# Routing of a mixture-of-experts layer: logits turned inside the second gate, the exponential ahead of the gate's activation, and row scatters sorted by choice

## The reference, cut to what matters

```python
logits = h @ gate_weight.T                              # 1024 tokens x 8 experts
scores = softmax(logits)
topk_w, topk_i = _group_limited_topk(scores)            # 2 of 4 groups of 2 experts, then 2 experts
wmat = (one_hot(topk_i, 8) * topk_w[..., None]).sum(axis=1)
e = einsum('ntf,nhf->nth', silu(h @ gate_w.T) * (h @ up_w.T), down_w)   # 352 features in an expert
routed = einsum('nth,tn->th', e, wmat)
shared = silu(h @ sh_gate_w.T) * (h @ sh_up_w.T) @ sh_down_w.T          # 704 features
x = x + routed + shared
```

## Time and profile before

| what | us |
|---|---|
| median of 3 runs | 995.75 |
| lowest and highest | 992.85, 997.42 |
| time of the profiled execution | 995.74 |
| its span, first to last instruction | 993.9 |

### The profile page before, as it was taken

One profiled execution on the slowest core, in us unless ns is written; L12 is line 12 of the kernel. 1 busy time (PEld: TensorE's weight loads), 2 busy tenths in 40 slices (PEclk: granted clock), 3 DMA queues, 4 the chain that ended last, 5 costly groups with the idle time before them and its releaser, 6 DMA issues. The chain is left out here.

```text
span 993.9 us, 15940 instructions
## 1 busy us (share of the span) xinstructions
PE 953.2 (96%) x5497; PEld 804.0 (81%) x5497; DVE 526.2 (53%) x975; ACT 412.8 (42%) x956; POOL 451.6 (45%) x489
## 2 busy tenths in 40 slices
PE   6999977999999989999999999999999999999998
PEld 5777756888878867888888988777778999999997
DVE  5434468777888835445454223337786333333345
ACT  2434458777878724334322044463442122222111
POOL 2889856655667610000000402227705878993051
PEclk9999989999999999999999999999999999999999
DMA  7688713111111105222320014302043657671153
GB/s 252 204 271 261 222 46 96 43 38 38 44 32 39 48 2 189 84 85 85 95 96 22 11 43 143 123 14 91 2 146 125 225 179 238 197 221 63 44 159 106
DMA packets 79003, 109.92 MB, mean 111 GB/s; under 512 B 14224, under 2 KB 46992, under 8 KB 78928
## 3 DMA queue, kind: packets, MB, share of 16 engines
q1 hardware_dynamic: 66288, 82.18, 26.9%
q10 hardware_dynamic: 10080, 18.35, 5.2%
q0 software_dynamic: 2560, 8.39, 2.6%
HBM read 83.13 MB, written 25.77 MB: 110 GB/s over the span
## 5 line engine op out<-in xcount | busy, mean ns | idle before, releaser
L43 PE MATMUL psum<-second_xT_hi,second_w_hi 128*128 128x512 f32 x272 | 108.0, 397 | 4.4 <-PEq L74 2.9
L44 PE MATMUL psum<-second_xT_lo,second_w_hi 128*128 128x512 f32 x272 | 107.0, 393 | 0.0
L45 PE MATMUL psum<-second_xT_hi,second_w_lo 128*128 128x512 f32 x272 | 106.9, 393 | 0.0
L1283 POOL TENSOR_TENSOR all_x<-all_x,mlp_raw 128x512 f32<-128x512 f32 x8 | 10.0, 1290 | 175.9 <-DVE all_x L1786 175.9
L2320 ACT ACTIVATE moe_s<-psum 128x352 f32<-128x352 f32 x39 | 18.1, 465 | 151.9 <-PE psum L45 151.9
L43 PEld LDWEIGHTS psum<-second_xT_hi,second_w_hi 128*128 128x128 f32 x272 | 51.7, 190 | 17.3 <-issue 3.7
L1741 ACT ACTIVATE mlp_s<-psum,mlp_side 128x512 f32<-128x512 f32 x32 | 21.8, 681 | 100.3 <-PE psum L45 100.3
L43 PE MATMUL psum<-moe_w_hi,moe_tT_hi 128*128 (+1 forms) x187 | 62.6, 335 | 0.0
L2391 DVE TENSOR_TENSOR moe_hT_lo<-psum,moe_hT_hi 128x384 fp32r<-128x384 f32 x38 | 21.2, 558 | 74.6 <-ACT moe_hT_hi L2327 74.6
L1786 DVE TENSOR_TENSOR all_x<-all_x,psum 128x512 f32<-128x512 f32 x64 | 43.8, 686 | 31.8 <-PE psum L45 31.3
L45 PEld LDWEIGHTS psum<-second_xT_hi,second_w_lo 128*128 128x128 f32 x272 | 51.6, 190 | 11.0
(11 more groups left out here) (346 smaller groups left out, 2848.9 us busy)
## 6 DMA issues: line engine op xcount, KB each, us to landing
kv_all<-all_x ACTq DMA_DIRECT2D x28, 256.0 KB
far_raw<-in_eg SPq DMA_DIRECT2D x10, 704.0 KB, 4.3
far_raw<-in_eu SPq DMA_DIRECT2D x10, 704.0 KB, 4.5
slot_rows<-mix_W SPq DMA_DIRECT2D x23, 256.0 KB, 5.8
slot_out<-far_rows ACTq DMA_DIRECT2D x23, 256.0 KB, 2.3
far_raw<-in_ed SPq DMA_DIRECT2D x10, 512.0 KB, 4.3
far_rows<-slot_rows ACTq DMA_DIRECT2D x19, 256.0 KB, 3.3
second_raw<-in_w_feat SPq DMA_DIRECT2D x18, 256.0 KB, 3.4
```

The source lines that it names most:

```text
L43: e.matmul(out, hi_l, hi_r, start=first, stop=False)
L44: e.matmul(out, hi_l, lo_r, start=False, stop=False)
L45: return e.matmul(out, lo_l, hi_r, start=False, stop=last)
L1283: pool.tensor_tensor(g["x"][:, t, :], g["x"][:, t, :], b2, ALU.add).then_inc(x_plus, 1)
```

## The change

It edits the order of work in the first three iterations of the loop and the order of the scatters. No operation is added but one: the cast of the slots is made in two parts, one for each choice, and the scatters of the first choice wait for the first part alone.

- PE: `turn_hidden(0)` stands ahead of `gate(1)` instead of behind it, and `tensor_logits` stands in the middle of `gate(1)` instead of behind `turn_hidden(0)`.
- ACT: `hidden_hi(0)` and the exponential stand ahead of `gated(1)`, and `hidden_hi(1)` ahead of `gated(2)`.
- DVE: the maximum and the subtraction stand ahead of `hidden_lo(0)`, the rest of part 0 (now part 7) behind it. `keep_results(0)` moves from behind part 2 to behind `product(2)`, one iteration later. Part 3 moves from behind `product(2)` to ahead of it.
- POOL: all eight tiles by the first choice, then all eight by the second.

```diff
@@ route_programs, vector
             link(v.tensor_tensor(lg[:], logits, per_tile(best[:], NE), ALU.subtract))
+        if m == 7:
             v.wait_ge(exp_ok, 1)
@@ m == 3
+            v.tensor_copy(slot[:, 0, :], slot_f[:, 0, :]).then_inc(slot_ok, 1)
             link(v.tensor_tensor(held[:], pos[:], chosen[:], ALU.mult))
             link(v.tensor_reduce(slot_f[:, 1, :], held[:], AX_X, ALU.max))
-            v.tensor_copy(slot[:], slot_f[:]).then_inc(slot_ok, 1)
+            v.tensor_copy(slot[:, 1, :], slot_f[:, 1, :]).then_inc(slot_ok, 1)
@@ phase_experts, gpsimd
-            pool.wait_ge(route.slot_ok, 1)
             pool.wait_ge(norm.normed, TT)
-            for t in range(TT):
-                for i in range(TOP):
+            for i in range(TOP):
+                pool.wait_ge(route.slot_ok, i + 1)
+                for t in range(TT):
@@ tensor, gate
-                features(j, 0, GB).then_inc(g_ready, 1)
+                if j == 1:
+                    features(j, 0, GB, range(DC // 2))
+                    route.tensor_logits(pe)
+                    features(j, 0, GB, range(DC // 2, DC)).then_inc(g_ready, 1)
+                else:
+                    features(j, 0, GB).then_inc(g_ready, 1)
@@ tensor, loop
+            pe.wait_ge(scan.o_ok, TT)
+            turn_hidden(0)
             for j in range(STEPS):
                 if j + 1 < STEPS:
                     gate(j + 1)
-                if j == 0:
-
-                    pe.wait_ge(scan.o_ok, TT)
-                if j < STEPS - 1:
+                if 0 < j < STEPS - 1:
                     turn_hidden(j)
-                if j == 0:
-                    route.tensor_logits(pe)
@@ scalar, loop
+                if j < 2:
+                    hidden_hi(j)
+                if j == 0:
+                    route.scalar(act)
                 if j + 1 < STEPS:
                     gated(j + 1)
-                if j == 0:
-                    hidden_hi(0)
-                    route.scalar(act)
@@ vector, loop
-            later = {0: 2, 1: 3, 2: 6, 3: 5}
+            later = {0: 2, 2: 6, 3: 5}
+                if j == 0:
+                    route.vector(v, 0)
                 if j < STEPS - 1:
                     hidden_lo(j)
                 if j == 0:
-                    route.vector(v, 0)
+                    route.vector(v, 7)
                     route.vector(v, 1)
+                if j == 1:
+                    route.vector(v, 3)
                 if j + 1 < STEPS:
                     product(j + 1)
+                if j == 1:
+                    keep_results(0)
```

More of the change, by code:

```diff
@@ L2226, in find_weights, with features @@
                         pe.wait_ge(w_ok, NW * LAST)
-            def features(j, i, bank):
+            def features(j, i, bank, these=range(DC)):
                 hi, lo = tokens(j)
-                for dc in range(DC):
+                for dc in these:
                     m = passes(pe, psum[:, bank + j % 2, 0:FE], hi[:, dc, :], lo[:, dc, :],
@@ L2361, in _ @@
             for j in range(STEPS):
+                if j < 2:
+                    hidden_hi(j)
+                if j == 0:
+                    route.scalar(act)
                 if j + 1 < STEPS:
                     gated(j + 1)
-                if j == 0:
-                    hidden_hi(0)
-                    route.scalar(act)
                 if routed(j - 1):
                     store_results(j - 1 - TT)
-                if j:
+                if j >= 2:
                     hidden_hi(j)
@@ L2475, in _ @@
                     hidden_lo(STEPS - 1)
-                keep_results(j)
+                if j:
+                    keep_results(j)
 def second_columns(nc, ctx, tag):
```

## The result

| | before | changed |
|---|---|---|
| median of 20 runs each, in turn on the same chip | 997.36 | 994.63 |
| lowest and highest | 992.85, 998.86 | 990.0, 996.87 |
| span of the profiled execution | 993.9 | 989.8 |

The ratio of the times is 0.9971, with a 95% interval of 0.9960 to 0.9982: the change wins 1.8 to 4.0 us, by the ratio 2.9. The forecast was 1.97 us and a time of 993.8. So the sign is as predicted, both values are within 0.5% of before as forecast, and the predicted gain is inside the interval, near its lower end.

A forecast was written before the change was run, and what follows sets the result against it. PE, busy 953.2 of 993.9 us, was taken as the bound. 1.37 us from the exponential and 0.60 from `keep_results(0)` make 1.97, so 995.74 - 1.97 = 993.8 us, range 991.4 to 996.4.

The forecast's parts named there:

- PE's stop between `up(2)` and `down(1)`: PE from 747.48 to 750.55 us: 2.04 us idle, the rest small matmuls; an edit of 3 us at most.
- The exponential, 1.37 us: On ACT, moved ahead of the silu: ends at 739.43 instead of 740.80, 1.37 us earlier.
- `keep_results(0)`, 0.60 us: On DVE, moved out of the row ahead of the low half of the hidden tile: 0.60 us more.
- Sum: `down(1)` starts at 748.58 instead of 750.55, 1.97 us earlier from the exponential and `keep_results(0)`.
- PE's own readiness: PE ready for `down(1)` by 748.46, with at most 0.44 + 0.43 us for the small matmuls; within 0.1 us of the low half.
- The ends of 1.6 and 2.2 us: Bounds of the 1.97 us gain; 2.2 from PE's readiness at 747.48 + 0.87 = 748.35 against 750.55.
- The logits' transposes: On PE inside `gate(1)`: input comes only 0.1 us before PE; idle time over 0.3 us ahead would show the prediction wrong.
- `product(2)` behind part 3: On DVE: `product(2)` runs from 751.3 to 751.85, 0.84 us to spare before `turn_hidden(2)`, so it costs nothing.
- The rival's price with part 3 alone: Slower rival, `product(2)` too late because DVE operations slow down: 996.0 with part 3 alone; chance 0.04.
- The scatters: On POOL: first choice's cast ends at 750.6, rows 2.9 us earlier, margin grows by 0.9; order itself given nothing.
- Drain at the table load: Rival on ACT: a drain is paid, the exponential ends 1.38 us later, 0.6 us won, 995.1; chance 0.02.
- The whole time: Profiled execution 995.74 - 1.97 = 993.8 us, span about 991.9; chance 0.79.

The follow-up runs named there:

- e1_exp_only: Changed kernel with `keep_results(0)` and part 3 put back where they were; 17.17 us from the first logits' last matmul to `turn_hidden(2)`.
- e2_keep_only: Kernel before with only `keep_results(0)` moved behind `product(2)`; 18.03 us from the first logits' last matmul to `turn_hidden(2)`.
- e6_low_inside: Changed kernel with hidden tile 1's low half ahead of the counts, small matmuls inside `down(1)`, `masked` in part 5; ratio to before 0.9969, median 1011.15 us.
- e0_before_again: Kernel before run again unedited on chip 0; ratio against itself 0.9998, median 1014.49 us.
- e9_wait_order: Changed kernel with POOL's two waits in the old order, slots then normed rows; first scatter 0.31 us behind the first cast, 16.57 us to `turn_hidden(2)`.
- e7_before_fourth: Kernel before, unedited, one more profile on chip 10; 18.63 us from the first logits' last matmul to `turn_hidden(2)`.
- e7_before_third: Kernel before, unedited, one more profile on chip 10; 20.21 us from the first logits' last matmul to `turn_hidden(2)`.
- e5_late_product: Changed kernel with four useless DVE operations behind the second cast; 18.47 us from the first logits' last matmul to `turn_hidden(2)`.
- e0_after_again: Changed kernel run again unedited on chip 0; ratio to before 0.9975, median 1012.02 us.

## Why the prediction was right, step by step

- **PE's stop between `up(2)` and `down(1)` is what can be won.** Right. PE's idle time there went from 2.04 to 0.41 us, and on the first chip nothing later took it back: from `turn_hidden(2)` to the end both kernels take 236.1 us. On the later chips a longer and varying stage lies in between.
- **The exponential, 1.37 us.** Right to 0.01 us in its end (739.43 against 737.47 + 1.96). Its part in the whole was 1.45 us by e1_exp_only. The 0.08 more are links of DVE: the logits' sum started 0.03 us behind the exponential (737.50 against 737.47), where before it was 0.11 us behind (740.91 against 740.80).
- **`keep_results(0)`, 0.60 us.** Right, 0.59 by e2_keep_only.
- **Sum.** 1.97 forecast, 2.05 measured in place.
- **PE's own readiness.** The bound of 0.87 us for the two small matmuls was too wide: without waits the second starts 0.17 us behind the first, and in e6_low_inside both take 0.36 us (747.99 to 748.35). So PE was ready at some 745.9, not within 0.1 us of the low half, and there was 0.5 us more to win, which e6_low_inside takes. The ends of 1.6 and 2.2 us rested on that.
- **The logits' transposes.** PE had no idle time in the profile's sense; they start 0.25 us behind the matmul ahead of them (735.45 to 735.70) instead of 0.16. What stands ahead of the stop costs nothing, as assumed.
- **`product(2)` behind part 3.** Right: no wait, a margin of 1.04 against 0.84 forecast. Part 3 took 2.75 us (746.40 to 749.15) where 2.87 was assumed. The rival's price with part 3 alone was added up wrongly: 993.8 + 12 x 0.23 - 0.84 is 995.7, not 996.0.
- **The scatters.** The slots of the first choice were ready as forecast (748.56 + 1.96 = 750.52, forecast 750.6). Then this part failed twice, without a price. The first scatter started at 751.41 in the old kernel's times instead of about 750.9, because the change also turned the order of two waits, which I had read as neutral. And the read back came only 1.97 us earlier, not 2.9, because of this and because the 15 steps from the first to the last scatter took 20.34 us instead of 19.96. So the margin ahead of PE's first turning of rows did not grow by 0.9 us; it stayed the same within 0.1 us and sufficed.
- **Drain at the table load.** The rival that pays one is out: the load starts 0.02 us behind the hidden tile (735.90 to 735.92) and the exponential 0.01 behind the load. The Trainium skill, "ScalarE: Activation LUTs", What ACT_TABLE_LOAD costs, has about 1283 ns for the load, which the trace repeats, and about 1380 ns of drain, which no row here shows.
- **The whole time.** The forecast of 993.8 us came within 0.8 us of the measured 994.63 partly by luck: it started from a median of three runs, 995.75, where twenty gave 997.36, and the gain was larger than forecast, two errors of opposite sign. The forecast span of 991.9 us against the measured 989.8 was off by the clock at 371 us. The measured gain by the ratio (2.9 us, and 2.5 on chip 0) is above the 2.05 in place, though both intervals contain that. What the prediction left out is the clock. If a stop of 3 us lowers it in half of the executions at a price of 1.57 us (20.19 against 18.62), the change wins 0.8 us more on average, 2.85 us in all. This estimate would fit, but it rests on six profiles, and the first chip's one showed no fall, so the excess stays open.

## What to carry to other kernels

In a kernel that one engine bounds, follow the releasers back from that engine's stop to the first operation that waited for something that it doesn't need. Here an exponential stood behind a silu that stood behind a whole gate, and its start could be moved by reordering alone, to 0.01 us of the forecast. Measure an edit of 2 us from an anchor in the trace ahead of it and not by the spans. When the order of waits is edited along the way, read it as a change too.

## What the runs showed that I had not expected

**The order of two waits before an indirect transfer is worth 0.57 us.** With the slots' semaphore first and the long-fulfilled one of the rows next to the transfer, the scatter starts 0.31 us behind the end of the cast (before, e0_before_again, e2_keep_only, both e7, e9_wait_order); the other way round it is 0.88 to 0.89 us (the other eight profiles). What in the sequencer takes that time stays open.

**A stop of PE may cost more than itself.** Behind the same 3 us the granted clock was 1.00 over the next 4 us in three profiles and 0.64 to 0.66 in three others. Chip 10 has both, with the same program (e7_before_fourth and e7_before_third).

**On the later chips the engines stand still for a part of the scatters.** From the first scatter (755.02) to 778 us in e0_before_again PE was busy for 16.9 of 23 us, on the first chip for all of 24:

```profile
755.00:778.00 23.00, 16.89 (x85) 15.32 (x83) 5.53 (x18) 3.26 (x6) 15.77 (x16) 0.87 0.48 182
```

```profile
752.00:776.00 24.00, 24.00 (x141) 22.51 (x141) 13.07 (x39) 4.84 (x10) 17.61 (x17) 1.00 0.51 185
```

The first fence is e0_before_again, the second the kernel before. In the waits of e0_before_again in this stage two of the longest are put down to no engine of the core (`remote`):

```profile
DVE moe_h L2386 <- remote: 9.6, 1, 9.6
...
ACT moe_s L2320 <- remote: 8.1, 1, 8.1
```

From `turn_hidden(2)` to the first turning of rows the later chips took between 35.3 us (e5_late_product) and 39.6 us (e6_low_inside), where the first chip had 27.4 and 27.3. The two kernels that come late to `turn_hidden(2)` are at the short end (35.3 both, with 35.4 for e9_wait_order and 38.7 for e0_after_again), so their delay of 1.9 us isn't seen in their times; whether coming late is what shortens the stage can't be said, as e9_wait_order doesn't come late. What holds the engines was not tried and stays open.
